# Interleaving gathered rounds and dense units by half rounds of four groups in a seven-pass graph network kernel

## The chip, the cores and the metric

The kernel runs as one program on one core of a Trainium2 chip. The metric is device time in microseconds (us) of one execution, the median of three runs. The engines are PE (matrix multiply), DVE (vector), ACT (scalar), POOL (gathers) and SP (issues transfers); each runs its own instruction stream and they meet at semaphores.

## The reference, cut to what matters

Four graph layers over 12500 nodes of 64 features and 200000 edges sorted by destination; each is followed by a residual and a layer norm:

```
x = _layernorm(x + L0(x))    # attention over edges, 4 heads
x = _layernorm(x + L1(x))    # per-node standard deviation of x[src]
x = _layernorm(x + L2(x))    # sum of x[src] + edges @ We, then an MLP
x = _layernorm(x + L3(x))    # four sage convolutions in a row
# sage_conv:
msg = x[src]
agg = jax.ops.segment_sum(msg, dst, num_segments=N_NODES)
deg = jax.ops.segment_sum(ones, dst, num_segments=N_NODES)
return (agg / maximum(deg, 1)) @ Wl.T + bl + x @ Wr.T
```

What the change touches is `segment_sum(x[src], dst)` in five passes: L1 ("dev") and the four convolutions ("sage1" to "sage4"). Destinations are crowded at low node numbers (`dst = 12500 * u**2`), so the upper half of the nodes receives only about 29% of the edges.

## The kernel before, in words

Nodes lie in 98 tiles of 128. Edges lie in 49 rounds of 8 groups of 512 edges. There are seven passes: gat, dev, gine, sage1, sage2, sage3, sage4. The passes gat and gine gather every round. Before dev, a matrix of edge counts (49 destination tiles by 98 source tiles, each 128x128, bf16) is built in DRAM.

The passes dev and sage1 to sage4 (`pass_dense`) work in two ways at once:

- **Dense unit.** For each of the 49 lower destination tiles, PE multiplies the 98 count tiles of that row by the node values (L921): 49 matmuls into one PSUM half (half 0), 49 into the other (half 1). SP keeps loading count tiles into a ring that holds exactly one unit, in 8 pieces; a piece is loaded again once its matmuls are done. DVE reduces each half (L1746) and adds it to the accumulator (L1750), in `take_dense`. In dev the unit is 28 + 21 matmuls, and the units run a second time over the other half of the sources.
- **Gathered (cold) round.** The last 15 rounds, whose edges go to the upper tiles, are gathered by POOL with indirect transfers into 8 slots (L620). For every pair of a group and a destination tile, DVE makes a one-hot matrix (L1700), PE multiplies (L949, 12 matmuls) into one of two PSUM banks, and DVE adds the sum of the pair before (L1707). A slot is handed back by DVE's index copy (L1695). The 15 rounds have 169 pairs in each pass, so about 11 in a round.

The order of the two is written in the program and depends on tables in SBUF that DVE computes once (L1657 to L1674). The outer loop has 7 steps ("blocks") of 7 units; at its end two blocks of nodes are processed (`node_vector` on DVE, `node_tensor` on PE, normalisation and the rows for the next pass; in dev one). TARGETS says how many rounds must be done at the end of each step, TURNS how many are done before each unit. After every unit, PE and DVE each load two values of TURNS into registers (L430, L431) and run the rounds between them (`cold_rounds`). On DVE the rounds stand between half 0 and half 1 of a unit: `take_dense(t, u, 0)`, the rounds, `take_dense(t, u, 1)`. The first group of four in a round loads eight registers of group spans (L425), the fifth does so again.

With the gains of the steps of 3, 3, 2, 2, 2, 2 and 1 rounds, the runs of units between rounds are 3, 2, 2 in the first two steps, 4, 3 in the next four, and 7 in the last. The last round of a step stands directly before its node work.

Of the kernel before, what the change touches and what calls it, by code (L numbers as in the profile page):

```python
# [15 lines left out]
P = 128  # L16
# [9 lines left out]
C = 4  # L26
# [58 lines left out]
def build(nc, x, edge_attr, src_r, dst_r, dst_b, src_c, dst_c, w, out):  # L85
    ctx = ExitStack()
    with ctx:
# [159 lines left out]
        TURNS = sb("TURNS", [P, KT + 1], I32)  # L247
# [180 lines left out]
        def cold_rounds(eng, u, r0, cold_round):  # L428

            first = eng.value_load(TURNS[0:1, bass.ds(u, 1)], min_val=0, max_val=ROUNDS)  # L430
            upto = eng.value_load(TURNS[0:1, bass.ds(u + 1, 1)], min_val=0, max_val=ROUNDS)  # L431
            with eng.If(first < upto):
                with eng.Fori(first, upto) as l:
                    cold_round(nc.s_assert_within(l + r0, 0, ROUNDS - 1, skip_runtime_bounds_check_because="upto <= ROUNDS - r0"))
# [277 lines left out]
        def _(pe):  # L712
# [193 lines left out]
            arrived = pe.alloc_register("pe_arrived")  # L906
# [18 lines left out]
            def pass_dense(k):  # L925
# [5 lines left out]
                def cold_round(r):  # L931

                    pe.reg_add(arrived, arrived, 16 * C)
                    for s in range(SLOTS):
# [21 lines left out]
                if dev:  # L956
# [4 lines left out]
                    for half in range(2):  # L961
                        pe.wait_ge(xp_loaded, 16 * (xp_before[k] + half + 1))
                        with pe.Fori(0, KT) as u:
                            dense_unit(k, u, u + half * KT, SRC_HALF)
                            if half == 0:
                                cold_rounds(pe, u, r0, cold_round)
                    return
                pe.wait_ge(xp_loaded, 16 * (xp_before[k] + xp_loads[k]))
                with pe.Fori(0, STEPS) as b:
                    with pe.Fori(0, TB) as r:  # L970
                        u = b * TB + r
                        dense_unit(k, u, u, TILES)
                        cold_rounds(pe, u, r0, cold_round)
                    node_tensor(pe, k, b * 2)
                    node_tensor(pe, k, b * 2 + 1)
# [275 lines left out]
        def _(ve):  # L1251
# [319 lines left out]
            def build_vector():  # L1571
# [93 lines left out]
                shares = tmp[:, 0, 0:KT].rearrange("p (b r) -> p b r", b=STEPS)  # L1665
                shares_i = tmp[:, 1, 0:KT].bitcast(I32)
                for r in range(TB):
                    step(ve.tensor_scalar(shares[:, :, r], gain, float(r * 9363), None, ALU.mult))
                step(ve.tensor_copy(shares_i, tmp[:, 0, 0:KT]))
                step(ve.tensor_scalar(shares_i, shares_i, 16, None, ALU.arith_shift_right))  # L1670
                step(ve.tensor_copy(tmp[:, 0, 0:KT], shares_i))
                step(ve.tensor_tensor(shares, shares, TARGETS[:, 0:STEPS].unsqueeze(2).broadcast_to([P, STEPS, TB]), ALU.add))
                step(ve.tensor_copy(TURNS[:, 0:KT], tmp[:, 0, 0:KT]))
                step(ve.tensor_copy(TURNS[:, KT:KT + 1], TARGETS[:, STEPS:STEPS + 1]))  # L1674
# [8 lines left out]
            prev, after = ve.alloc_register("ve_prev"), ve.alloc_register("ve_after")  # L1683

            def pass_dense(k):
# [23 lines left out]
                def cold_round(r):  # L1709

                    for s in range(SLOTS):
# [42 lines left out]
                def unit(t, u, rounds):  # L1754

                    take_dense(t, u, 0)
                    if rounds:
                        cold_rounds(ve, t, r0, cold_round)
                    take_dense(t, u, 1)

                for s in range(SLOTS - 1):
                    take_indices(s, r0 * SLOTS + s)
                if name == "dev":
                    with ve.Fori(0, STEPS) as b:
                        step.loop(b, per + 1)
                        with ve.Fori(0, TB) as r:
                            unit(b * TB + r, b * TB + r, True)
# [3 lines left out]
                    with ve.Fori(0, STEPS) as b:  # L1771
                        step.loop(b, per)
                        with ve.Fori(0, TB) as r:
                            unit(b * TB + r, b * TB + r + KT, False)
# [58 lines left out]
```

## Time and profile before

| what | us |
|---|---|
| median of 3 runs | 12794.58 (12789.05 to 12804.66) |
| profiled execution | 12813.53 |
| its span | 12811.7 |
| dev, its first 49 units with the 15 rounds | 5829 to 6658 |
| sage1 / sage2 / sage3 / sage4 | 9189 / 10205 / 10979 / 11938 to the end |

The profile counts an engine busy only while it computes. Register loads, branches and semaphore waits are idle time: an idle stretch that ends with "issue" is one in which the engine's own sequencer was at work. A row of the timeline gives start, length, engine, line, operation, operands, count, and in brackets the idle time before it with what ended it.

### The profile page before, as it was taken

How to read it: one execution, taken by the hardware profiler on the slowest of the kernel's cores; microseconds unless marked ns; L12 is line 12 of the kernel's file. 1: busy time of each engine (PE TensorE's matmuls, PEld its weight loads, DVE VectorE, ACT ScalarE, POOL GpSimd, SP SyncE). 2: the span in 40 equal slices, each digit the busy share in tenths (PEclk: the TensorE clock that was granted, in tenths of full speed). 3: DMA queues.
4: the chain of work that ended last, by engine and by line, in shares of the span. 5: the costliest groups of instructions: out<-in, count | busy, mean ns of one | idle time of the engine just before them, and what ended most of it. 6: DMA issues, size and time to landing. Idle time of an engine off the chain costs nothing.

```text
span 12811.7 us, 273411 instructions
## 1 busy us (share of the span) xinstructions
PE 7656.7 (60%) x61727; PEld 5494.5 (43%) x61728; DVE 5118.7 (40%) x13474; ACT 1761.8 (14%) x3566; POOL 5615.3 (44%) x5555
## 2 busy tenths in 40 slices
PE   5666666663665555556788444444566655455666
PEld 4555555552112222224455333444555544444566
DVE  4444545546544444443433222333322233322333
ACT  2333333331012222330000000000000000000000
POOL 4666555452000000005530577777654376554554
PEclk7777777776555555557889655566677766666777
DMA  2222222221001111115555322222455566655666
GB/s 59 66 63 63 64 62 61 61 59 36 20 40 54 66 70 70 70 80 169 150 169 176 75 51 56 56 58 58 121 189 173 198 206 232 217 183 199 203 216 202
DMA packets 977744, 1416.34 MB, mean 111 GB/s; under 512 B 540705, under 2 KB 649761, under 8 KB 970914
## 3 DMA queue, kind: packets, MB, share of 16 engines
q1 hardware_dynamic: 689858, 1130.79, 26.0%
q0 software_dynamic: 184832, 224.29, 9.0%
q10 hardware_dynamic: 102752, 58.62, 1.6%
q14 instruction: 281, 2.30, 0.1%
q8 instruction: 21, 0.34, 0.0%
HBM read 1197.73 MB, written 215.36 MB: 110 GB/s over the span
## 4 chain that ended last, share of the span: by engine, by line
PE 31%; issue 23%; DVE 14%; DVEq 14%; POOL 9%; DMA 6%; ACT 1%; SPq 1%; POOLq 0%; ACTq 0%
PE ps_turn L921 13%; POOL ARENA L620 9%; PE ps_turn L884 7%; PE ps_out L776 4%; DMA ARENA<-table_gat,idx 2%; DMA ARENA<-counts 2%; DVE onehots L1700 2%; DVEq L1714 2%; PE ps_pair L776 1%; DMA idx<-src_r 1%; DVEq L392 1%; PE ps_turn L692 1%; PE ps_pair L949 1%; DVE ARENA L1635 1%; DVEq L1630 1%
## 5 line engine op out<-in xcount | busy, mean ns | idle before, releaser
L620 POOL DMA_INDIRECT ARENA<-table_sage,idx x1920 | 1901.7, 990 | 1729.5 <-DVE idx L1695 1192.8
L921 PE MATMUL ps_turn<-ARENA 128*128 128x96 bf16 (+2 forms) x24010 | 2274.4, 262 | 543.0 <-DVE DSUM L1746 215.9
L921 PEld LDWEIGHTS ps_turn<-ARENA 128*128 128x128 bf16 x24010 | 1864.0, 106 | 948.7 <-issue 647.7
L884 PE MATMUL ps_turn<-ARENA 128*128 x3736 | 1515.8, 508 | 1219.5 <-issue 584.4
L620 POOL DMA_INDIRECT ARENA<-table_gat,idx x1568 | 1671.9, 1066 | 1188.1 <-issue 1131.0
L620 POOL DMA_INDIRECT ARENA<-table_gine,idx x1568 | 1541.2, 983 | 964.1 <-issue 950.1
L620 POOL DMA_INDIRECT ARENA<-table_dev,idx x480 | 481.8, 1004 | 2660.0 <-DVE idx L1695 2522.3
L1635 DVE TENSOR_SCALAR ARENA<-ARENA 128x784 f16 x1868 | 902.6, 483 | 1415.9 <-PE ps_turn L884 963.9
L949 PE MATMUL ps_pair<-ARENA,onehots 128*128 128x32 bf16 (+2 forms) x10140 | 699.7, 227 | 997.4 <-DVE ARENA L1707 868.6
L776 PE MATMUL ps_out<-ARENA,onehots 128*128 128x256 f32 (+1 forms) x3136 | 950.0, 472 | 517.7 <-DMA ARENA<-table_gine,idx 368.9
L884 PEld LDWEIGHTS ps_turn<-ARENA 128*128 x3736 | 389.1, 104 | 1959.0 <-issue 1863.2
L776 PE MATMUL ps_pair<-ARENA,onehots 128*128 128x256 f32 (+1 forms) x3136 | 882.5, 446 | 389.1 <-DMA ARENA<-table_gine,idx 303.4
L949 PEld LDWEIGHTS ps_pair<-ARENA,onehots 128*128 x10140 | 574.0, 117 | 1128.3 <-issue 1127.1
L776 PEld LDWEIGHTS ps_out<-ARENA,onehots 128*128 128x128 f32 x3136 | 724.1, 286 | 631.5 <-issue 555.5
L1073 ACT ACTIVATE ARENA<-ps_turn 128x784 f32 x784 | 645.4, 823 | 2112.9 <-PE ps_turn L902 2112.9
L1746 DVE TENSOR_REDUCE DSUM<-ps_turn 128x128 f32<-128x384 f32 (+2 forms) x588 | 230.0, 391 | 1756.2 <-PE ps_turn L921 1643.5
L1700 DVE SCALAR_TENSOR_TENSOR onehots<-DST,TBASE,COL 128x512 f32 x845 | 637.0, 754 | 640.0 <-issue 639.5
L776 PEld LDWEIGHTS ps_pair<-ARENA,onehots 128*128 128x128 f32 x3136 | 677.8, 269 | 493.9 <-issue 429.3
L1030 ACT ACTIVATE bigT<-ps_turn 128x896 f32<-128x896 f32 (+1 forms) x42 | 38.4, 915 | 3454.3 <-PE ps_turn L685 3454.3
L1450 DVE TENSOR_TENSOR ARENA<-ARENA,ps_out 128x261 f32 (+1 forms) x584 | 205.7, 354 | 761.8 <-PE ps_out L776 761.3
L1018 ACT ACTIVATE tmp<-COL,dst_in 128x128 bf16<-128x128 f32 x1568 | 495.3, 386 | 0.0
L776 PE MATMUL ps_out<-ARENA,tmp 128*128 128x256 f32 (+1 forms) x1536 | 417.2, 435 | 128.0 <-DVE tmp L1444 126.2
(298 smaller groups left out, 6850.4 us busy)
## 6 DMA issues: line engine op xcount, KB each, us to landing
ARENA<-counts SPq DMA_DIRECT2D x1470, 448.0 KB
counts<-ARENA SPq DMA_DIRECT2D x49, 3136.0 KB, 9.0
ARENA<-counts SPq DMA_DIRECT2D x490, 224.0 KB
ARENA<-dst_b SPq DMA_DIRECT2D x393, 256.0 KB
ARENA<-edge_attr SPq DMA_DIRECT2D x390, 128.0 KB, 2.5
ARENA<-table_sage,idx POOLq DMA_INDIRECT x1920
ARENA<-table_gat,idx POOLq DMA_INDIRECT x1568
ARENA<-table_gine,idx POOLq DMA_INDIRECT x1568
```

Of the source, the lines that this page charges most:

```text
L620: pool.indirect_dma_start(ps["buf"][:, s, c, 0:ps["row"]], None, ps["table"][:, :], bass.IndirectOffsetOnAxis(idx[:, s, c:c + 1], 0)).then ...
L776: last = pe.matmul(sums[:, 0:H * D if gat else n], lhs, rhs, start=(c == 0 and q == 0), stop=(c == C - 1 and q == parts - 1))
L884: last = pe.matmul(ps_turn[:, at:at + WIDE_ROW // 2], ring[:, 0:P], ring[:, P + q * (WIDE_ROW // 2):P + (q + 1) * (WIDE_ROW // 2)], start= ...
L921: last = pe.matmul(ps_dense[half][:, 0:n], RING[:, b, :], XP[:, b, :], start=(b == PIECE_AT[pieces[0]]), stop=(j == pieces[-1] and b == PI ...
L949: last = pe.matmul(sums, hot[:, c * P:(c + 1) * P], buf[:, s, c, q * n:(q + 1) * n], start=(c == 0 and q == 0), stop=(c == C - 1 and q == 2))
L1018: act.activation(distance[:, c * P:(c + 1) * P], COL[:, :], ACT.Abs, scale=-1.0, bias=dst_in[:, s % 2, c:c + 1]).then_inc(hot_distance, 1)
L1073: act.activation(to[:, :, c * CHUNK:(c + 1) * CHUNK].rearrange("p (q b) v -> p q b v", q=2), sums.rearrange("p q (b v) -> p q b v", v=CHUN ...
L1450: return ve.tensor_tensor(a, a, ps_sums[q][:, 0:n].unsqueeze(1), ALU.add)
L1635: ve.tensor_scalar(ring[:, P:P + WIDE_ROW], IOTA16, BASES[:, bass.ds(i * 4 + c, 1)], KEY[:, bass.ds(j, 1)], ALU.add, ALU.is_equal).then_in ...
L1700: return ve.scalar_tensor_tensor(ring, DST[:, bass.ds(cols, C)].unsqueeze(2).broadcast_to([P, C, P]), TBASE[:, bass.ds(t, 1)], COL[:, :].u ...
L1714: with ve.Fori(lo, hi) as t:
L1746: ve.tensor_reduce(DSUM[:, half, 0:n], ps_dense[half][:, 0:3 * n].rearrange("p (q v) -> p v q", q=3), X_AXIS, ALU.add).then_inc(dense_read, 1)
```

## The change

`cold_rounds` is replaced by `dense_step`, which runs one outer step. TURNS has an entry for each half round (98 entries): how many units precede it. Each half round loads its entry, runs the units up to it, then runs four groups. The step starts by loading two entries of TARGETS_I and ends with the units that are left. On DVE a unit is now whole: both halves are taken, then come groups. By the new table the half rounds stand after 1, 2, 3, 4, 5 and 7 units in a step of 3 rounds, after 1, 3, 5 and 7 in a step of 2, and after 3 and 7 in a step of 1. There are thus 30 stretches of gathered work in a pass where there were 15.

```diff
-        def cold_rounds(eng, u, r0, cold_round):
-            first = eng.value_load(TURNS[0:1, bass.ds(u, 1)], ...)
-            upto = eng.value_load(TURNS[0:1, bass.ds(u + 1, 1)], ...)
-            with eng.If(first < upto):
-                with eng.Fori(first, upto) as l:
-                    cold_round(... l + r0 ...)
+        def dense_step(eng, b, done, r0, dense_unit, cold_groups):
+            def units(upto):
+                now = eng.snap(done, min_val=0, max_val=KT)
+                with eng.If(now < upto):
+                    with eng.Fori(now, upto) as u:
+                        dense_unit(... u ...)
+                    eng.reg_mov(done, upto)
+            first = eng.value_load(TARGETS_I[0:1, bass.ds(b, 1)], ...)
+            upto = eng.value_load(TARGETS_I[0:1, bass.ds(b + 1, 1)], ...)
+            with eng.If(first < upto):
+                with eng.Fori(first, upto) as l:
+                    for half in range(2):
+                        units(eng.value_load(TURNS[0:1, bass.ds(l * 2 + half, 1)], ...))
+                        cold_groups(r, range(half * SLOTS // 2, (half + 1) * SLOTS // 2))
+            units(b * TB + TB)
...
 # PE, in the outer loop over b (dev alike)
-                    with pe.Fori(0, TB) as r:
-                        u = b * TB + r
-                        dense_unit(k, u, u, TILES)
-                        cold_rounds(pe, u, r0, cold_round)
+                    dense_step(pe, b, done, r0, lambda u: dense_unit(k, u, u, TILES), cold_groups)
...
 # DVE
-                def unit(t, u, rounds):
+                def unit(t, u):
                     take_dense(t, u, 0)
-                    if rounds:
-                        cold_rounds(ve, t, r0, cold_round)
                     take_dense(t, u, 1)
...
 # the table, on DVE
-                for r in range(TB):
-                    step(ve.tensor_scalar(shares[:, :, r], gain, float(r * 9363), None, ALU.mult))
+                for b in range(STEPS):
+                    step(ve.tensor_scalar(shares[:, b, :], COL[:, 0:2 * ROUNDS], begin[:, b:b + 1], rate[:, b:b + 1], ALU.subtract, ALU.mult))
...
```

DVE, sage4, from the reading of the first half of a unit to the first load of a gathered round, before. DSUM is the reduced half, ps_turn the PSUM of the dense halves, SPAN the table of tiles of each group; piece_used_3 is signalled by PE at the end of half 0.

```order
1862 L1746 TENSOR_REDUCE DSUM<-ps_turn 128x64 [waits piece_used_3]
1863 L1747 ISA
1864 L1750 ISA [waits dense_read]
1865 L1750 SCALAR_TENSOR_TENSOR ARENA<-DSUM,FLAG,ARENA 128x64
1866 L1751 REGISTER_ALU
1867 L430 ISA [waits dense_added]
1868 L430 TENSOR_LOAD TURNS
...
1871 L431 TENSOR_LOAD TURNS
...
1876 L425 TENSOR_LOAD SPAN
```

The same place of the changed kernel; piece_used_7 is signalled by PE at the end of half 1.

```order
2045 L1768 REGISTER_ALU [waits dense_added]
2046 L1770 TENSOR_REDUCE DSUM<-ps_turn 128x64 [waits piece_used_7]
2047 L1771 REGISTER_ALU
2048 L1774 SCALAR_TENSOR_TENSOR ARENA<-DSUM,FLAG,ARENA 128x64 [waits dense_read]
2049 L1775 REGISTER_ALU
2050 L434 REGISTER_ALU [waits dense_added]
2051 L434 COMPARE_AND_BRANCH
2052 L433 UNCONDITIONAL_BRANCH
2053 L426 ISA
2054 L426 TENSOR_LOAD SPAN
```

Gathered work on DVE moved from behind the reading of half 0 to behind the reading of half 1, and the two loads of TURNS between are gone.

PE, sage4, from the last matmuls of a unit to the wait for the first one-hot, before. The semaphore pair_hot is signalled by DVE's one-hot, gathered_3_0 by the gather.

```order
1483 L921 MATMUL ps_turn<-ARENA 128x192 x6
1484 L430 ISA
1485 L430 TENSOR_LOAD TURNS
...
1488 L431 TENSOR_LOAD TURNS
...
1493 L425 TENSOR_LOAD SPAN
1494 L404 ISA
1495 L938 UNCONDITIONAL_BRANCH [waits gathered_3_0]
1496 L939 ISA
1497 L945 ISA [waits pair_hot,pair_acc]
```

The middle of a round in the changed kernel, where dense units now stand between the fourth group and the fifth:

```order
1781 L952 COMPARE_AND_BRANCH
1782 L445 ISA
1783 L445 TENSOR_LOAD TURNS
...
1785 L433 COMPARE_AND_BRANCH
1786 L434 UNCONDITIONAL_BRANCH
1787 L434 ISA
1788 L931 ISA [waits dense_read]
...
1806 L934 MATMUL ps_turn<-ARENA 128x192 x6
1807 L434 REGISTER_ALU
1808 L434 COMPARE_AND_BRANCH
...
1811 L426 TENSOR_LOAD SPAN
```

On PE the two loads after every unit are gone, and one load stands after every four groups.

## Rows read from the trace of the kernel before

**Rows 1.** The page: chain that ended last, by engine
```profile
PE 31%; issue 23%; DVE 14%; DVEq 14%; POOL 9%; DMA 6%; ACT 1%; SPq 1%; POOLq 0%; ACTq 0%
```

**Rows 2.** Windows: start:end, us, busy us (count) by engine, PEclk, DMA share, GB/s
```profile
5829.00:6658.00 829.00, 629.79 (x4429) 410.68 (x4427) 340.99 (x780) 4.71 (x12) 481.76 (x480) 0.82 0.54 160
...
10205.00:10979.00 774.00, 400.83 (x6830) 366.84 (x6827) 257.23 (x739) 13.27 (x42) 476.42 (x481) 0.69 0.66 228
```

**Rows 3.** Waits from 5829: who waited for whom, total, times, longest
```profile
PE ps_pair L949 <- DVE ARENA L1707: 868.6, 748, 3.3
```

**Rows 4.** Timeline of PE, sage4, two stretches of units and one round
```profile
12338.10 11.05 PE L921 MATMUL ps_turn<-ARENA 128*128 128x192 bf16 x98 [1.60 <-issue]
12353.36 9.90 PE L921 MATMUL ps_turn<-ARENA 128*128 128x192 bf16 x98 [4.21 <-DVE DSUM L1746]
...
12393.73 0.82 PE L949 MATMUL ps_pair<-ARENA,onehots 128*128 128x64 bf16 x12 [1.72 <-DVE ARENA L1707]
...
12404.63 10.24 PE L921 MATMUL ps_turn<-ARENA 128*128 128x192 bf16 x98 [1.21 <-issue]
12416.02 8.24 PE L921 MATMUL ps_turn<-ARENA 128*128 128x192 bf16 x98 [1.16 <-DVE DSUM L1746]
...
12435.69 0.73 PE L949 MATMUL ps_pair<-ARENA,onehots 128*128 128x64 bf16 x12 [2.04 <-issue]
```

**Rows 5.** Timeline of DVE, sage4, end of a unit and start of a round
```profile
12424.42 0.36 DVE L1746 TENSOR_REDUCE DSUM<-ps_turn 128x64 f32<-128x192 f32 x1 [3.16 <-PE ps_turn L921]
12424.92 0.28 DVE L1750 SCALAR_TENSOR_TENSOR ARENA<-DSUM,FLAG,ARENA 128x64 f32 x1
...
12430.36 0.28 DVE L1750 SCALAR_TENSOR_TENSOR ARENA<-DSUM,FLAG,ARENA 128x64 f32 x1 [0.24 <-DVE DSUM L1746]
12433.72 0.75 DVE L1700 SCALAR_TENSOR_TENSOR onehots<-DST,TBASE,COL 128x512 f32 x1 [3.07 <-issue]
```

**Rows 6.** The lines of the register loads: count, ns min/median/max
```profile
L430 DVEq FUSED_REGOPS  x490: 46/132/224, 5837.8 to 12769.9; - x164
...
L430 DVEq TENSOR_LOAD <-TURNS x245: 300/312/849, 5837.9 to 12769.6; - x123
...
L425 DVEq TENSOR_LOAD <-SPAN x150: 594/605/628, 5855.6 to 12783.2; - x150
```

**Rows 7.** Windows in sage4: a steady unit, a round, the start of the next units
```profile
12374.00:12384.00 10.00, 8.03 (x98) 7.80 (x95) 2.05 (x6) 0.00 (x0) 0.00 (x0) 1.00 0.96 315
12388.00:12404.00 16.00, 6.80 (x101) 5.40 (x98) 9.20 (x24) 0.00 (x0) 12.32 (x13) 0.50 0.18 37
12404.60:12409.60 5.00, 4.97 (x37) 4.66 (x38) 0.00 (x0) 0.00 (x0) 3.78 (x5) 0.58 0.38 93
```

**Rows 8.** Timeline of PE, dev, three units and a round
```profile
6280.19 24.85 PE L921 MATMUL ps_turn<-ARENA 128*128 128x384 bf16 x147 [0.45 <-issue]
6307.22 0.84 PE L949 MATMUL ps_pair<-ARENA,onehots 128*128 128x128 bf16 x12 [2.19 <-DVE ARENA L1707]
...
6319.92 1.46 PE L949 MATMUL ps_pair<-ARENA,onehots 128*128 128x128 bf16 x12 [1.75 <-DVE ARENA L1707]
```

**Rows 9.** Timeline of PE, sage3, two units between rounds
```profile
11181.76 6.67 PE L921 MATMUL ps_turn<-ARENA 128*128 128x96 bf16 x98 [1.35 <-issue]
...
11199.37 0.65 PE L949 MATMUL ps_pair<-ARENA,onehots 128*128 128x32 bf16 x12 [3.24 <-DVE onehots L1700]
```

**Rows 10.** Timeline of PE, sage3, first units of a step of four and three
```profile
11418.09 4.72 PE L921 MATMUL ps_turn<-ARENA 128*128 128x96 bf16 x98
...
11448.15 1.06 PE L921 MATMUL ps_turn<-ARENA 128*128 128x96 bf16 x21 [0.38 <-DMA ARENA<-counts]
```

**Rows 11.** Timeline of DVE before dev: the old table
```profile
5810.01 1.42 DVE L1668 TENSOR_SCALAR tmp<-small 128x7 f32<-128x7 f32 x7
```

**Rows 12.** DMA queues, gat (1000:1400): packets, MB, share
```profile
q14 instruction: 37, 0.30, 0.3%
```

**Rows 13.** DMA queues, sage2 (10205:10979)
```profile
q14 instruction: 4, 0.03, 0.0%
```

More of the change, by code:

```diff
@@ L246, in build @@
         INFO = sb("INFO", [P, 2], I32)
-        TURNS = sb("TURNS", [P, KT + 1], I32)
+        TARGETS_I = sb("TARGETS_I", [P, STEPS + 1], I32)
+        TURNS = sb("TURNS", [P, 2 * ROUNDS], I32)
         rangev = sb("rangev", [P, 2 * H])
@@ L905, in _ @@
             seen, turn, bank = pe.alloc_register("pe_pair"), pe.alloc_register("pe_turn"), pe.alloc_register("pe_bank")
-            arrived = pe.alloc_register("pe_arrived")
+            arrived, done = pe.alloc_register("pe_arrived"), pe.alloc_register("pe_done")
             def dense_unit(k, t, u, srcs):
@@ L929, in pass_dense, with cold_groups @@
                 dev = ps["name"] == "dev"
-                def cold_round(r):
-                    pe.reg_add(arrived, arrived, 16 * C)
-                    for s in range(SLOTS):
+                def cold_groups(r, slots):
+                    if slots[0] == 0:
+                        pe.reg_add(arrived, arrived, 16 * C)
+                    for s in slots:
                         lo, hi = load_four(pe, spans, s, r * SLOTS + s)
@@ L1683, in _ @@
             prev, after = ve.alloc_register("ve_prev"), ve.alloc_register("ve_after")
+            done = ve.alloc_register("ve_done")
             def pass_dense(k):
@@ L1707, in add, with cold_groups @@
                     return ve.tensor_tensor(a, a, ps_pair[:, bass.ds(ve.snap(bank, min_val=0, max_val=512), n)].unsqueeze(1), ALU.add)
-                def cold_round(r):
-                    for s in range(SLOTS):
+                def cold_groups(r, slots):
+                    for s in slots:
                         g = r * SLOTS + s
@@ L1762, in pass_dense @@
                     take_indices(s, r0 * SLOTS + s)
+                ve.reg_mov(done, 0)
                 if name == "dev":
@@ L1765, in pass_dense @@
                         step.loop(b, per + 1)
-                        with ve.Fori(0, TB) as r:
-                            unit(b * TB + r, b * TB + r, True)
+                        dense_step(ve, b, done, r0, lambda u: unit(u, u), cold_groups)
                         flush()
@@ L1773, in pass_dense @@
                         with ve.Fori(0, TB) as r:
-                            unit(b * TB + r, b * TB + r + KT, False)
+                            unit(b * TB + r, b * TB + r + KT)
                         node_vector(ve, step, k, split, b + STEPS, b)
@@ L1779, in pass_dense @@
                     step.loop(b, 2 * per + 1)
-                    with ve.Fori(0, TB) as r:
-                        unit(b * TB + r, b * TB + r, True)
+                    dense_step(ve, b, done, r0, lambda u: unit(u, u), cold_groups)
                     flush()
```

45 lines of the change are left out of this document (30 added, 15 removed).

## The prediction

> **What bounds the kernel now.** I read the chain that ended last first [rows 1]: PE has 31%, and issue and DVE's sequencer another 37%. No engine and no transfer is full, so time goes into hand-overs between PE and DVE. Then the windows by pass [rows 2]: in dev PE is busy 630 of 829 us, in sage2 401 of 774, and POOL, whose 480 gathers are the fixed work of a pass, 482 and 476. So POOL has some 300 us of idle time in either. In the list of waits [rows 3] PE's gathered matmuls wait for DVE's additions (868.6 us): PE and DVE take turns there at some 1.8 us a pair, and no gather is waited for. So the order of the work matters only through what a switch between dense and gathered work costs, and what it hides.
>
> The timeline of PE shows a switch [rows 4]. A steady unit of sage4 takes 8.24 us and the next starts 1.16 us later. After the last unit of a run the first gathered matmuls come 2.04 us later, and after a round the next unit comes 1.21 us later and takes 10.24 us instead of 8.24. DVE's side [rows 5]: it reads half 0, loads the table, and makes the first one-hot from 12433.72, while PE's unit runs to 12425.41 + 8.24 = 12433.65 (the unit after the row of 12416.02). The one-hot is done by 12434.47, PE is ready for it at 12435.69. The preparation of DVE is thus hidden behind half 1 of the unit. This cover the change takes away: DVE now reads half 1, which exists only when PE has stopped, before it makes the first one-hot.
>
> **The change part by part.** Per pass there are 30 stretches of gathered work where there were 15; 7 still end a step. All times are of the profiled execution.
>
> *Entry of a gathered stretch, after.* In sage4, from PE's end of the unit (T = 12416.02 + 8.24 = 12424.26): DVE starts the reduction at T + 0.16, and its addition ends at T + 0.94 [rows 5]. From that point to a one-hot it was 3.07 us of issue, in which stood two loads of TURNS. One is a load of 0.31 us, two register operations of 0.13 and the steps between, about 0.75 [rows 6]; without two of them 1.6 us are left. The one-hot takes 0.75, and PE needs about 0.5 from there to its first matmul. Sum 0.94 + 1.6 + 0.75 + 0.5 = 3.8 us, against 2.04. For dev, whose reduction and addition are 0.25 us longer together, 4.05 against 2.19 [rows 8]. For sage2 and sage3, with shorter ones, 3.65 against 3.24 [rows 9]. No row shows this entry as such. Below, it is no shorter than the old one, if something hides the chain; above, I allow 1.2 us more, which is the extra idle of DVE's path if the register work of the new loops is as long as that of a load pair. I take the sums, as each part has a row.
>
> *Exit.* One load of TURNS now stands behind every four groups: 1.21 + 0.75 = 2.0 us in the sage passes, 0.45 + 0.8 = 1.3 in dev [rows 4, 8].
>
> *Middle of a round.* It had an idle time of 1.72 us, in which both engines load spans [rows 4], 1.75 in dev [rows 8] (about 2.0 in sage3). A new switch replaces it, so it is subtracted.
>
> *Slow first unit.* [...] A half round with its two gaps is still some 14 us in which PE does little, so I charge the 2.0 us at each new switch. In dev three units of 49 + 49 half matmuls after a round took 24.85 us [rows 8], 0.8 above three times 8.0.
>
> New switches, 15 in each pass: sage1 and sage4 3.8 + 2.0 - 1.75 + 2.0 = 6.05, so 91 us each. Dev 4.05 + 1.3 - 1.65 + 0.8 = 4.5, so 68. Sage2 and sage3 3.65 + 2.1 - 2.0 = 3.75, so 56 each (their unit times come below).
>
> Old entries, 15 in each pass, grow by 1.8 (sage1, sage4: 27), 1.85 (dev: 28) and 0.45 (7). The 8 old exits inside steps grow by 0.75: 6 us a pass.
>
> *Start of a step.* Two loads of TARGETS_I and one of TURNS, 2.3 us on PE and on DVE, 7 times: 16 us a pass. Where PE's first unit is hidden behind DVE's node work (sage4: PE waits until 12353.36 [rows 4]) it is DVE's loads that count, and the price is the same.
>
> *What is saved.* Inside a run of units PE's pause of 1.16 us [rows 4] is mostly its two loads. There were 34 such pauses in a pass and are 19, which I put at 0.2: sage1 saves 35 us, sage4 27, since 7 of its pauses lie behind node work. In dev the pause does not show (24.85 for three units). In sage2 and sage3 the units of a long run wait for the ring: in sage3 four units took 31.1 us (11418.09 to 11449.2) [rows 10], the first of them 4.72 of computing, and two units between rounds 14.4 (11181.76 to 11199.37 - 3.24) [rows 9]. During a half round the ring fills, so a run of one costs 5.0 at the start of a step and 6.3 elsewhere (6.67 in the row), a run of two 14.4. A step of two rounds then has 5 + 3 x 14.4 = 48.2 where it had 31.1 and, for three units, a time between 31.1 and 14.4, about 24: 55. Four such steps save 28, the two of three rounds about 9 each: 46 us a pass. This is the one real gain, a fuller ring.
>
> *The table.* It took 2.8 us; seven operations of 0.20 [rows 11] stay seven, but several over 686 columns come in. I put 5 us (0 to 15), on the path before dev.
>
> Sum: sage1 91 + 27 + 6 + 16 - 35 = 105; sage4 113; dev 68 + 28 + 6 + 16 = 118; sage2 and sage3 56 + 7 + 6 + 16 - 46 = 39 each; table 5. Together 419 us. The profiled execution took 12813.5, so 13232; it was 0.15% above the median of the runs, so the time on their scale is 13213 us, 3.3% slower.
>
> **The rivals.**
> *A. Most of the chain stays hidden, or the clock holds.* If the entries stay as they were, the new and old ones together cost 2 x (27 + 27 + 28 + 7 + 7) = 192 us less: 13020. If the first units after a half round keep the high clock, as a shorter pause might allow, 72 us less: 13140. For it: the clock in the round of [rows 7] is low only because PE is nearly idle. Against: the dependence on half 1 is in the program's order.
> *B. Not slower.* The finer order fills the ring and spreads the gathers; every switch is free. Then what is left is the saving: 35 + 27 + 2 x 46 = 154 us against 80 for the steps' starts, 30 for the exits and 5 for the table, about 12760. It decides only if DVE had time to make the one-hot before PE ends half 1, and DVE cannot pass its own wait for half 1.
> *C. Code loading.* The block loop on DVE grows, since the unit stands in it three times. In the gat pass, whose loop on DVE is longer than that of any other pass, the instruction queue moved 37 packets in 400 us [rows 12]; in sage2, 4 in 774 us [rows 13]. If the new loop behaved as that of gat, each of the 35 steps would load anew, at a few packets and perhaps 2 to 4 us: 70 to 140 us more, 13280 to 13350.
> [...]
> *D. The table does not spread the half rounds*, for instance by its rounding. Then both halves follow one another and only the old entries, the loads and the table are paid: some 96 + 80 + 5 + 15 x 5 x 0.75 = 237, less 120 saved in pauses: 12920.
>
> [...]
>
> **How the numbers follow.** Forecast as summed 0.72, A 0.12 (between 13020 and 13140), B 0.04, C 0.07, D 0.05. The forecast's own error is a fifth of its 420 us, and the bounds of the entries (192 us down, 1.2 x 150 = 180 up) are rarely reached whole. The range is 13050 to 13350 us. About 0.2% is what a measurement of this kernel can tell from no change. Faster by more has 0.04 (B), within it 0.02 (a part of B or D), slower 0.94.
>
> **What would show it right or wrong.** Of the profile of the changed kernel I expect: 30 stretches of L963 in each pass; idle time of PE before the first of each of 3.6 to 4.1 us, ended by DVE's one-hot; in sage4 about 2 us before the units after it and 10 us for the first; runs of units with pauses near 0.2 in sage1; sage2 and sage3 longer by some 40 us, dev, sage1 and sage4 by 105 to 118. POOL's gathers stay 480 a pass and are hardly waited for. It is wrong if the entries stay near 2 us, if the first units after a half round take 8.2, if instruction packets appear in the sage passes, or if PE waits for gathers in the steps of three rounds, where four groups are asked for every 21 to 25 us (6.3 or 10.2 for the unit, a switch, half a round) and POOL has 16 us of work for them (16 gathers of 1.0 us, 482 over 480 in [rows 2]) besides its gaps.

## The result and the profile after

| | us |
|---|---|
| before, median of 4 runs | 12792.9 (12789.05 to 12804.66) |
| after, median of 4 runs | 13296.22 (13287.02 to 13300.2) |
| ratio after/before | 1.0391 (95% interval 1.0373 to 1.0409) |
| profiled span, before / after | 12811.7 / 13296.3 |

The change makes the kernel 3.9% slower. The forecast was 13213, 3.3%. The windows of the changed kernel, one for each pass (dev first half, dev second half, gine, sage1, sage2, sage3, sage4); the columns are those of [rows 2]:

```profile
5838.80:6815.00 976.20, 696.42 (x4429) 449.27 (x4430) 342.37 (x776) 4.70 (x12) 478.65 (x480) 0.73 0.45 135
6815.00:7293.00 478.00, 408.01 (x2402) 239.66 (x2402) 174.84 (x350) 6.28 (x16) 8.30 (x9) 0.92 0.57 169
7293.00:9361.30 2068.30, 952.00 (x4255) 828.00 (x4254) 620.98 (x1222) 50.96 (x84) 1546.37 (x1563) 0.58 0.26 58
9361.30:10467.50 1106.20, 709.86 (x7180) 629.41 (x7180) 289.22 (x753) 40.20 (x70) 471.64 (x482) 0.71 0.51 170
10467.50:11291.80 824.30, 412.39 (x6830) 378.11 (x6830) 256.20 (x739) 13.27 (x42) 476.15 (x481) 0.67 0.63 214
11291.80:12292.40 1000.60, 518.78 (x7180) 440.34 (x7181) 279.22 (x753) 47.97 (x70) 477.60 (x480) 0.65 0.54 184
12292.40:13296.00 1003.60, 605.26 (x6830) 562.95 (x6830) 323.15 (x815) 2.92 (x14) 478.41 (x478) 0.72 0.54 181
```

The same windows of before are 829.2, 482.0, 2049.2, 1015.6, 774.2, 959.0 and 873.0 us. So dev grew by 147, sage1 by 91, sage2 by 50, sage3 by 42, sage4 by 131. What runs ahead of dev took 10 more (5839 for 5829), but it takes between 5823 and 5842 in the profiles of the experiments on like chips, so the 5 us of the table can't be told. Gine, whose code is untouched, grew by 19. DVE and POOL are as busy as before (dev 341 and 482 in [rows 2]); PE is busier with the same number of matmuls, at a lower mean clock (0.73 in dev, where [rows 2] have 0.82). The rest is waiting. Two rows of the waits from 5839 on:

```profile
DVE DSUM L1770 <- PE ps_turn L934: 2147.9, 517, 10.4
PE ps_pair L963 <- DVE ARENA L1731: 1273.8, 749, 15.7
```

The second was 868.6 us in 748 waits [rows 3]. The first was, in the kernel before, from 5829 on:

```profile
DVE DSUM L1746 <- PE ps_turn L921: 1643.5, 446, 8.9
```

DVE waits 504 us more for PE, in 71 more waits, and PE 405 us more for DVE's additions, in as many waits as before. The timeline of PE in sage1, one full cycle of a half round and two units, answers to [rows 4]:

```profile
10210.96 0.82 PE L963 MATMUL ps_pair<-ARENA,onehots 128*128 128x64 bf16 x12 [1.16 <-DVE ARENA L1731]
10213.40 18.12 PE L934 MATMUL ps_turn<-ARENA 128*128 128x192 bf16 x196 [1.63 <-issue]
10235.33 0.82 PE L963 MATMUL ps_pair<-ARENA,onehots 128*128 128x64 bf16 x12 [3.81 <-DVE ARENA L1731]
10236.90 0.82 PE L963 MATMUL ps_pair<-ARENA,onehots 128*128 128x64 bf16 x12 [0.74 <-DVE ARENA L1731]
```

The entry is 3.81 us (forecast 3.8, before 2.04), and the exit 1.63 (forecast 2.0, before 1.21). The exit differs from place to place: the next one in the same view is 2.07, and the median of sage1 is 1.62. Two units take 18.12 as one run without a pause between them. DVE's side of the same entry answers to [rows 5]:

```profile
10231.67 0.36 DVE L1770 TENSOR_REDUCE DSUM<-ps_turn 128x64 f32<-128x192 f32 x1 [3.29 <-PE ps_turn L934]
10232.18 0.28 DVE L1774 SCALAR_TENSOR_TENSOR ARENA<-DSUM,FLAG,ARENA 128x64 f32 x1
10234.11 0.75 DVE L1724 SCALAR_TENSOR_TENSOR onehots<-DST,TBASE,COL 128x512 f32 x1 [1.65 <-issue]
```

PE ends its unit at 10213.40 + 18.12 = 10231.52. DVE starts the reduction 0.15 later, ends the addition at + 0.94, issues for 1.65 (forecast 1.6), and the one-hot takes 0.75; PE starts at + 3.81. This chain lay behind half 1 before.

### The profile page after: what moved, and what is told of

Same layout as the page of the kernel before. It is cut to its first block, busy times and chain, and to the rows that moved or that the text cites. A ratio compares the mean times of both kernels' runs of the same rounds, so it can differ in the third digit from the quotient of the medians.

```text
span 13296.3 us, 271981 instructions
## 1 busy us (share of the span) xinstructions
PE 7812.0 (59%) x61727; PEld 5616.2 (42%) x61728; DVE 5118.0 (38%) x13480; ACT 1761.9 (13%) x3566; POOL 5623.4 (42%) x5555
## 4 chain that ended last, share of the span: by engine, by line
PE 33%; issue 23%; DVE 14%; DVEq 13%; POOL 9%; DMA 6%; ACT 1%; SPq 1%; POOLq 0%; ACTq 0%
PE ps_turn L934 14%; POOL ARENA L633 9%; PE ps_turn L897 7%; PE ps_out L789 4%; DMA ARENA<-table_gat,idx 2%; DMA ARENA<-counts 2%; DVE onehots L1724 2%; PE ps_pair L963 2%; DVEq L1738 2%; PE ps_pair L789 1%; DMA idx<-src_r 1%; PE ps_turn L705 1%; DVE ARENA L1650 1%; DVEq L393 1%; DVEq L1645 1%
## 5 line engine op out<-in xcount | busy, mean ns | idle before, releaser
L934 PE MATMUL ps_turn<-ARENA 128*128 128x96 bf16 (+2 forms) x24010 | 2387.7, 270 | 535.4 <-issue 366.0
L934 PEld LDWEIGHTS ps_turn<-ARENA 128*128 128x128 bf16 x24010 | 1949.9, 109 | 963.3 <-issue 664.8
L963 PE MATMUL ps_pair<-ARENA,onehots 128*128 128x32 bf16 (+2 forms) x10140 | 741.0, 234 | 1324.0 <-DVE ARENA L1731 1273.8
L963 PEld LDWEIGHTS ps_pair<-ARENA,onehots 128*128 x10140 | 608.8, 121 | 1467.1 <-issue 1465.1
```

The costliest lines, as they stand in the source:

```text
L934: last = pe.matmul(ps_dense[half][:, 0:n], RING[:, b, :], XP[:, b, :], start=(b == PIECE_AT[pieces[0]]), stop=(j == pieces[-1] and b == PI ...
L963: last = pe.matmul(sums, hot[:, c * P:(c + 1) * P], buf[:, s, c, q * n:(q + 1) * n], start=(c == 0 and q == 0), stop=(c == C - 1 and q == 2))
```

## Experiments

On one of the chips that served, the kernel before takes 16110 us (15964 in a second set of runs) instead of 12793; the first five experiments ran there. The gathered stretches of every kernel are torn there by pauses that the first chip does not have: in the third kernel below, from dev's last dense matmul to the first of sage1, a stretch that is almost all of gine and its gathers, it takes 2810 us where the kernel before has 2077 on the first chip; dev's second run of dense units, in which POOL gathers nothing, takes 452 and 455. In the kernel with DVE's old table and new order (third below) DVE's timeline in sage4 and its waits show one of them and their sum:

```profile
15214.33 0.22 DVE L1707 TENSOR_TENSOR ARENA<-ARENA,ps_pair  x1 [8.10 <-remote]
```

```profile
DVE ARENA L1707 <- remote: 1404.3, 206, 15.2
```

In the third kernel's 45 stretches of sage2 to sage4 the mean idle time of PE is 1.0 us before the second and third pair, 1.6 before the fourth, 4.0 before the fifth and 6.2 before the ninth, where the kernel before has 1.0 to 1.5 before each of the second to tenth in the four sage passes on the first chip. The pauses thus come mostly from the fourth or fifth pair of a stretch on, so they weigh on long stretches more than on short ones, and a ratio from there can't be carried to another chip: two kernels ran on both, and had 0.9832 and 0.9967 of the kernel before there, 1.0128 and 1.0327 elsewhere. The idle times between single instructions can: the new entry in sage1 has a median of 3.81 there, in the kernel with shifted code, and 3.83 on the first chip. From these five I use those; the seven others ran on chips where the kernel before takes 12803 and 12812 us.

**Half 1 behind the groups again.** Table, loops and 30 stretches stay as changed; DVE reads half 1 of the last unit only after the four groups.

```diff
-                        units(eng.value_load(TURNS[... l * 2 + half ...]))
-                        cold_groups(r, ...)
+                        goal = eng.value_load(TURNS[... l * 2 + half ...])
+                        with eng.If(now < goal):
+                            with eng.Fori(now, goal) as u:
+                                halves(u, 0)
+                                with eng.If(u + 1 < goal):
+                                    halves(u, 1)
+                        cold_groups(r, groups)
+                        with eng.If(now < goal):
+                            halves(kept, 1)
```

> The changed kernel, but on DVE the second half of the last unit before each half round is read behind the four groups, as in the kernel before; a unit index is kept in a register for it, and the code of DVE grows a little. Theory (the uncovered preparation on DVE is the largest part): the gaps between the end of a unit and the first gathered matmuls fall from 3.7 to 4.1 us to about 1.2 us (PE's own loads alone), 150 times, some 390 us less than the changed kernel: about 12900 us, between 12850 and 12980. Rival (the finer grain itself costs, by slow first units and exits): the gaps fall but the time stays above 13150. Rival (code loading on DVE): instruction packets grow further and eat 50 us or more of the gain.

15832.03 us, ratio 0.9832 (0.9811 to 0.9852) on the slow chip, so the expected 12900 can't be judged here; the tenth experiment does it. The medians of the entries were 1.03 in dev, 0.50 in sage1, 1.65 in sage2 and sage3, 0.52 in sage4, below the expected 1.2 in three passes and above it in two.

**Both half rounds at one place.** The changed kernel with a table that gives both halves of a round the same number of units: 15 stretches.

```diff
+                step(ve.tensor_copy(pairs_of[:, :, 0], pairs_of[:, :, 1]))
```

> The changed kernel, but the table gives both halves of a round the same number of units, so 15 stretches of gathered work stand in a pass and the code is the same. Theory: each of the 15 saved switches gives back 5.8 us in sage1 and sage4 (entry 3.8, exit 1.8, slow first unit 2.0, less 1.75 of idle time inside the round), 5.4 in dev, 3.75 in sage2 and sage3, 370 us in all, less 92 us that the fuller ring had given: about 13020 us. Rival (the order on DVE and the new loads are nearly all of it): 13200 or more. Rival (the ring's gain is not real): 12930.

16218.08 us, ratio 1.0069 (1.0045 to 1.0094) there, which decides neither for the expected 13020 nor for its rivals. The 15 entries kept the new length: 4.12, 3.83, 3.72, 3.84 and 3.85 us. The length of an entry is therefore not a matter of how often it comes, and the table of the change does spread the half rounds (30 stretches against 15): rival D falls.

**The order on DVE alone.** The kernel before, in which DVE reads half 1 ahead of the rounds.

```diff
                     take_dense(t, u, 0)
+                    take_dense(t, u, 1)
                     if rounds:
                         cold_rounds(ve, t, r0, cold_round)
-                    take_dense(t, u, 1)
```

> The kernel before, whole rounds and its own table, but DVE reads both halves of a unit before the rounds. Theory: the entry becomes 0.94 + 3.07 + 0.75 + 0.5 = 5.3 us in sage4 where it was 2.04, 3.3 us more 15 times in sage1, sage4 and dev, 1.9 more in sage2 and sage3: 206 us, about 13000 us. Rival (DVE's order is hidden by something else): within 30 us of the kernel before, 12793.

16295.88 us, ratio 1.0117 (1.0087 to 1.0147) there, which is 186 us. The medians of the entries are 5.50, 5.38, 5.12, 5.14 and 5.24, where the kernel before has 2.19, 2.04, 3.24, 3.23 and 2.02 on the first chip. The 75 entries add up to 396 us instead of 189, and the difference of 207 meets the expected 206; the time of the whole agrees, as far as a time from this chip can. One line that moves costs that much: with the two loads of TURNS still in the chain, an entry is 5.1 to 5.5 us; without them, as in the change, 3.8.

**Shifted code.** The changed kernel with 191 more instructions (semaphore increments) in a branch of DVE's program that is never taken, ahead of the building of the tables, so that DVE's loops from dev on stand 196 instructions further.

```diff
+                with ve.If(wide(ve) > 0):
+                    for _ in range(191):
+                        settle(ve)
```

> The changed kernel with 191 instructions on DVE that are never run (they stand in a branch that is not taken), ahead of the table building, so that all later loops of DVE stand elsewhere in the code. Theory (code loading is a part, which depends on where a loop stands): the 72 instruction packets of the gine pass and the 35 of sage4 go or change, gine falls by 19 us to the 2049 us that it took before, sage4 by up to 17: about 13260 us. Rival (gine and sage4 are longer for another reason): 13296 us, gine 2068, whatever the packets do.

16052.76 us, ratio 0.9967 (0.9955 to 0.9978) on the slow chip, where I had no run of the unchanged kernel to hold beside it: undecided. The instruction queue moved 285 packets where the changed kernel moves 379 and the kernel before 281.

**The loops with whole rounds and half 1 behind the groups.** The first two edits together, as a version that might beat both kernels.

> The changed kernel with the table of whole rounds (both halves of a round after the same units, so 15 stretches of gathered work) and, on DVE, the second half of the last unit before a round read behind its first four groups. The runs before this one had gaps at the entry of gathered work of 0.5 us with that cover (1.65 in sage2 and sage3), 3.8 without, where the kernel before has 2.0 (3.2). Theory (the hand-overs are the price, so whole rounds with the cover keep the saving of the loads and pay nothing): against the kernel before the entries give back 1.5 us 75 times (110 us), the pauses between units 60 us, and the starts of steps and the exits cost some 100 us: about 12720 us on a scale where the kernel before takes 12793, ratio 0.994 (0.985 to 1.003). Rival (the longer code of DVE or its branches eat it): a ratio of 1.005 or more.

15861.46 us, ratio 0.9945 (0.9927 to 0.9963). This met the number, but on the slow chip, and this kernel ran on no other. The half rounds with the same cover had 0.9832 there and 1.0128 elsewhere, so the number is not to be carried.

**The changed kernel again.** Unchanged, as the base for the next three.

> The changed kernel itself, unchanged, beside the kernel before on the chip on which the experiments run; it is the base for the others. On the first chip it took 1.0391 of the kernel before. If the pauses that stretch gathered work on the second chip fall on it as on the variant with the same half rounds (541 us against 1337 to 1444 us in the kernels with whole rounds), the ratio here is about 1.00 (15930 + 485 - 800 to 900 us: 0.97 to 1.00). If they do not depend on how long a stretch is, it is 1.03. Either way the medians of the entries should be 3.8 us in sage1 and sage4, 4.1 in dev, 3.7 in sage2 and sage3, and against the variant in which DVE reads half 1 behind the groups this one should be longer by the entries: some 30 x (2.2 x 2 + 3.0 + 2.0 + 3.3 - 2 x 0.5) or, from the medians of both, 30 x (3.1 + 3.3 + 2.1 + 2.1 + 3.3) = 417 us, less what the pair stretches took longer there (half 1 is still computing when the first pair comes), 200 to 300 us net.

13298.06 us (13283.93 to 13302.08) against 12803.36, ratio 1.0387 (1.0369 to 1.0404). This chip behaves as the first one; the ratio was expected for the slow one, and only the entries can be compared: 4.10, 3.82, 3.68, 3.75 and 3.82, as expected.

**Busier gathered stretches.** Three matmuls of 256 columns behind each pair, into a bank whose content is dead.

```diff
                             last.then_inc(pair_agg, 1)
+                            for _ in range(3):
+                                pe.matmul(ps_turn[:, 0:256], ZERO[:, :], ZEROS[:, 0:256], ...)
```

> The changed kernel with three more matmuls of 256 columns into a dead PSUM bank behind each pair on PE, so that PE is busier in a gathered stretch; nothing else is changed and the result of the extra work is not used. Theory (the slow first unit is the price of PE's idleness in the half round): the granted clock in the stretches rises, the first unit after a half round takes 8.3 instead of 10.5 us in sage1 and sage4 and about 8 instead of 10.2 in dev, and 5.9 instead of 6.1 in sage2 and sage3, so 90 x 2.1 = 190 us less, against at most 845 pairs x 0.3 to 0.6 us if the extra matmuls delay the next pair: between -190 and +300 us. Rival (the first unit is slow for another cause, such as count tiles that come late): its time stays at 10.5 and the kernel only gets longer by what the extra matmuls take. The length of a one-unit run is read in the trace, whatever the sum.

13199.61 us (13180.02 to 13206.26), ratio 1.0311 (1.0293 to 1.0328): 98 us less than the changed kernel in the same set. By pass dev gave 57, sage1 17, sage4 17, gine 7, sage2 and sage3 5 and 4. The first unit after a half round, median of all in a pass, fell from 10.01 to 8.12 us in dev, from 10.55 to 9.90 in sage1, from 10.29 to 9.90 in sage4 (9.93, 10.56 and 10.33 in the first profile of the changed kernel); in sage2 and sage3 it stayed at 6.2 to 6.4. The medians hide two kinds of units: 21 of 29 in dev and 9 of 29 in sage4 took 8.1 to 8.2 us, the others 9.4 to 11.0. So the expected 8.3 of sage1 and sage4 came for a part of the units alone, and 98 us of the 190 were won. A half round of dev and the first 3 us of the unit behind it, in the changed kernel:

```profile
6261.00:6273.00 12.00, 7.63 (x72) 6.16 (x72) 5.80 (x14) 0.00 (x0) 6.71 (x7) 0.64 0.15 41
6273.20:6276.20 3.00, 3.00 (x10) 1.46 (x11) 0.00 (x0) 0.00 (x0) 2.29 (x3) 0.50 0.29 86
```

The same with the three matmuls:

```profile
6443.00:6454.20 11.20, 8.11 (x75) 6.48 (x75) 4.60 (x11) 0.00 (x0) 8.27 (x8) 0.75 0.23 60
6454.30:6457.30 3.00, 3.00 (x19) 1.83 (x20) 0.00 (x0) 0.00 (x0) 2.09 (x4) 1.00 0.24 68
```

In 3 us PE does 10 matmuls at a granted clock of 0.50 and 19 at 1.00. The slow first unit is the clock: if the time of a first unit is multiplied by the mean granted clock in it, the product is 8.06 to 8.13 us for every one in dev and 8.14 to 8.25 for every one in sage1 and sage4, in the kernel before, in the changed one and with the matmuls, and PE has no idle time in one. Count tiles that come late would show as idle time, as the 0.38 before a run of 21 matmuls in [rows 10]. In sage2 and sage3 the product is 4.1 to 4.2 where the median unit takes 6.2 to 6.5, so the clock costs some 2.1 us there too, and with the three matmuls the clock of those half rounds was still 0.51 and 0.52 on average. The 57 us of dev are 41 less in the dense runs and 18 less in the gathered runs, with some 1 more in the idle times between them.

**The same in the kernel before.**

> The kernel before with the same three extra matmuls behind each pair. By the clock theory the first unit after a round falls from 10.24 to about 8.3 us in sage1 and sage4, 15 times in each, so half as much is won as in the changed kernel (some 60 to 90 us) at the same price for the pairs; the changed kernel gains by its larger number of first units. By the rival nothing is won.

12755.67 us (12745.58 to 12766.53, 6 runs), ratio 0.9962 (0.9949 to 0.9974): the only version that beats the kernel before on such a chip. A round of sage4 and the first 5 us of the unit behind it, and that unit in PE's timeline:

```profile
12388.00:12409.90 21.90, 15.06 (x177) 9.72 (x175) 11.92 (x32) 0.00 (x0) 15.20 (x15) 0.69 0.20 58
12410.00:12415.00 5.00, 5.00 (x61) 5.00 (x62) 4.21 (x8) 0.00 (x0) 3.92 (x4) 1.00 0.48 149
```

```profile
12305.41 10.13 PE L921 MATMUL ps_turn<-ARENA 128*128 128x192 bf16 x98 [7.01 <-DVE DSUM L1748]
...
12409.99 8.24 PE L921 MATMUL ps_turn<-ARENA 128*128 128x192 bf16 x98 [1.23 <-issue]
```

8.24 us instead of the 10.24 of [rows 4], at a clock of 1.00 instead of the 0.58 of [rows 7]. The price of the cold clock in a first unit was 2.0 us, as charged. In dev all 14 first units behind a round took 8.1, in sage4 8 of 14 took 8.2 and the others 9.7 to 10.6. The 48 us won are less than the 60 to 90 expected. Sage4 won only 6 us (dev 22, sage1 26), though its 14 first units had shrunk by 1.4 on average: behind node work PE arrives earlier and waits longer for DVE, 7.01 in the first row where [rows 4] have 4.21.

**Shifted code, beside the changed kernel.** The same kernel as the fourth, now in one set with its base.

> The changed kernel with 191 vector instructions in a branch that is never taken, ahead of the gine pass, so that the loops of gine and of sage1 to sage4 stand 196 instructions further in DVE's program; run once more, beside the unchanged kernel on the same chip. Theory (gine's 19 us more and a part of sage4's come from instructions loaded anew in every trip of a loop of about 300 instructions, 5 packets a trip, which depends on where the loop stands): gine is 15 to 25 us shorter than in the unchanged kernel, sage4 10 to 30 us, the instruction queue moves some 95 packets less, in all 20 to 50 us. Rival (gine's 19 us are something else, such as data that come later): the packets go and the time stays within 10 us.

13224.75 us (13215.62 to 13228.24), ratio 1.0327 (1.031 to 1.0344): 73 us less than the changed kernel, more than the 20 to 50 expected. The two profiled executions are 59 apart, of which gine is 20, sage4 36 and dev 7; dev has 2 instruction packets in both, so its 7 are not code loading. The instruction queue over the whole kernel, changed and then shifted:

```profile
q14 instruction: 379, 3.10, 0.1%
```

```profile
q14 instruction: 285, 2.33, 0.1%
```

In gine alone it was 69 packets, and 3 when shifted; in sage4 32, and 2. DVE's timeline at the start of a step of sage4 shows what they cost: the last operation of the node work and the next reduction, in the changed kernel of this set:

```profile
12448.59 0.62 DVE L1150 TENSOR_TENSOR X<-tmp,small 128x448 f32 x1
12460.98 0.36 DVE L1770 TENSOR_REDUCE DSUM<-ps_turn 128x64 f32<-128x192 f32 x1 [11.77 <-issue]
```

and shifted:

```profile
12426.63 0.62 DVE L1150 TENSOR_TENSOR X<-tmp,small 128x448 f32 x1
12430.82 0.36 DVE L1773 TENSOR_REDUCE DSUM<-ps_turn 128x64 f32<-128x192 f32 x1 [3.57 <-issue]
```

The same instructions, 8.2 us apart; PE had ended both halves of the unit at 12450.44 in the changed kernel, 10.5 us before the reduction. PE's first pair behind them shows it as an entry, changed and then shifted:

```profile
12465.92 0.82 PE L963 MATMUL ps_pair<-ARENA,onehots 128*128 128x64 bf16 x12 [15.48 <-DVE ARENA L1731]
```

```profile
12435.74 0.82 PE L963 MATMUL ps_pair<-ARENA,onehots 128*128 128x64 bf16 x12 [7.18 <-DVE ARENA L1734]
```

**Half 1 behind the groups, on a chip without the pauses.** The same kernel as the first.

> The changed kernel, but DVE reads half 1 of the last unit behind the four groups again, as the kernel before did: same table, same loops, 30 stretches a pass. Theory (the entries are the largest part of the loss): the entries, 665 us in the five passes of the changed kernel, fall to some 170 (medians 1.0 in dev, 0.5 in sage1 and sage4, 1.7 in sage2 and sage3, 30 each, plus those behind node work), and 30 to 100 us come back because the first pairs run while half 1 is still computed; so 400 to 470 us less than the unchanged changed kernel: 12830 to 12900 us, a ratio of 1.003 to 1.008 to the kernel before. Rival (loads, switches and the clock are the larger part): above 13000 us.

12972.91 us (12961.37 to 12980.23) against 12811.65, ratio 1.0128 (1.0111 to 1.0144). It is 325 us shorter than the changed kernel (whose median is from another chip, on which the kernel before is 8 us shorter), outside the 400 to 470 expected, and under the 13000 of the rival. The medians of the entries are as expected (1.01, 0.49, 1.61, 1.63, 0.49), and their sum over the five passes fell from 662 to 319, not to 170. The missing part is behind node work: five entries each of 12 to 14 us in sage2 and sage4, and of 8 in dev. Sage2 has 34 instruction packets in this kernel, where the changed kernel has 4, and sage4 33, where it has 32; gine has 3 for 69 and is 10 us shorter. In sage2 DVE's timeline shows the same hole as above, and PE's the entry:

```profile
10394.47 0.39 DVE L1173 TENSOR_TENSOR tmp<-big 128x224 f32<-128x224 f32 x1
10406.34 0.26 DVE L1786 TENSOR_REDUCE DSUM<-ps_turn 128x32 f32<-128x96 f32 x1 [11.48 <-issue]
```

```profile
10410.31 0.65 PE L979 MATMUL ps_pair<-ARENA,onehots 128*128 128x32 bf16 x12 [13.57 <-DVE ARENA L1747]
```

So the edit gave back what it should in sage1 (1007, before 1016) and sage3 (959, before 959), and came with its own code loading in sage2, which stayed at 830. Of the 161 us above the kernel before, sage2 has 56, dev 44 (first units still 9.80 us), sage4 40.

**That with the three matmuls.**

> The kernel of the run before with three more matmuls of 256 columns into a dead PSUM bank behind each gathered pair; their result is not used. Theory of the clock: with short entries PE idles less between a unit and the pairs, so the clock holds in dev as in the kernel before with these matmuls (first unit 8.1 us) and in sage1 and sage4 too (8.3 to 8.6 instead of 9.9): 60 to 150 us less than without them, 12700 to 12820 us. Rival (they delay the pairs when these overlap with half 1): no gain or a loss.

12889.47 us (12875.71 to 12890.89), ratio 1.0057 (1.0041 to 1.0074): 83 us less, by the theory, though above its 12820 since the base was higher. The first unit is 8.12 in dev, 10.16 in sage1 and 9.71 in sage4, where the theory said 8.3 to 8.6. As without the cover, 9 of the 29 in sage4 took 8.2 and the others 9.5 to 11.1, so the short entries did not change that.

**The same with both half rounds at one place.**

> The loops of the change, both half rounds of a round at one place by the table, half 1 read behind the groups, and the three extra matmuls: the best of all parts by the runs so far. Without the extra matmuls it was 0.9945 of the kernel before; with them the kernel before was 0.9962 of itself. If both add up, 0.990 to 0.992: 12680 to 12700 us.

12907.44 us (12887.19 to 12912.47), ratio 1.0069 (1.0052 to 1.0086). The expectation failed: 0.9945 had been measured where long stretches are torn by pauses, and it was wrong to multiply it with a ratio from another chip. Sage2 is at 829 and has 34 instruction packets here too. Between the last two kernels, which differ in the table alone, whole rounds are 18 us slower than half rounds. So in these loops the spreading of the half rounds costs nothing. That is not to say that the split is free against the kernel before: these loops pass from one kind of work to the other in the middle of every round, whether units stand there or not. PE's idle time in the middle of a whole round has a median of 3.4 to 4.1 us here by pass, where the kernel before with the same matmuls has 1.3 to 1.6, and the gathered runs of the five passes add up to 193 us more.

## Why the prediction was right, and where its numbers were not

The side, the mechanism and the range held. The terms stand beside what PE's timelines show, as sums of the idle times and runs of a pass (after minus before, forecast in brackets, in us):

| | entries | exits and step starts | gathered runs | dense runs | pass |
|---|---|---|---|---|---|
| dev | +111 (89) | +41 (42) | -6 (-25) | 0 (+12) | +147 (118) |
| sage1 | +84 (84) | +31 (52) | -25 (-26) | -6 (-5) | +91 (105) |
| sage2 | +66 (62) | +50 (54) | -25 (-30) | -43 (-46) | +50 (39) |
| sage3 | +75 (62) | +35 (54) | -28 (-30) | -39 (-46) | +42 (39) |
| sage4 | +141 (84) | +48 (52) | -26 (-26) | -32 (+3) | +131 (113) |

In sage1 and sage3 a step starts behind node work of PE. That work and the idle time behind it (+15 in sage1, +3 in sage3) are left out of the columns, though the forecasts in brackets hold 16 for the starts of steps. The passes differ from the sums of the columns by up to 7. The entries of sage4 hold about 36 us of code loading: with the shifted code they are +105.

- *Entries.* The chain of four parts came out at 3.8 in sage1 and sage4 and 3.7 in sage2 and sage3, and the change of DVE's order made it (third experiment, with the old loads still in the chain). This was most of the loss: with half 1 behind the groups 325 us of the 495 are gone (the placement of the code changed as well, which gave 10 back in gine). Rival A falls: in the changed kernel the entries did not stay hidden, and the first units did not keep the clock.
- *Slow first unit.* The 2.0 us of sage4 was right and is the clock: in sage4 of the kernel before the 14 first units behind a round took 9.55 to 11.05 us, and each multiplied by the mean granted clock in it gives 8.14 to 8.19. The term that was mis-sized is dev's: 0.8 a unit, read from three units that followed a whole round. The medians over all first units are 9.05 before and 9.93 after, against 8.12 at the full clock. So 29 x 1.8 - 15 x 0.9 = 39 us stand where I had 12. In the same way dev's gathered runs hardly shrank (-6 for -25). My reading took the clock of dev's rounds to stay as it was; before, it was 0.67 on average between the first pair of a round and the next unit, after, 0.51. The total of dev's dense runs hid this growth, by the next point.
- *Entries behind node work.* In the steps of sage4 and dev whose first stretch follows the first unit, that unit now runs while DVE still works on the nodes, and PE waits at the pair instead of at the next unit: 7.2 to 8.7 in sage4 without code loading, 7.4 to 8.7 in dev. The wait thus moved from the dense runs to the entries: sage4 has -32 for +3 there, and dev 0, though its first units alone added 39.
- *Fuller ring.* The one gain, -46 in sage2 and sage3, measured -43 and -39.
- *Code loading.* I had made it a rival of 0.07 and put it into each of the 35 steps at 2 to 4 us, for 13280 to 13350 us. The 37 packets of [rows 12] lie in seven rounds of gat (224 of its 1568 gathers), so 5.3 to a round, and by their share, 0.3% of 16 engines' 400 us, one took some 0.5 us, 2.6 a round. That a step would take 2 to 4 us longer was an estimate, and no run shows it: the first entry of five steps of sage4 took 14.4 to 15.5 us where it takes 7.2 to 8.7 with the shifted code, 5.9 to 8.3 more each, gine 20 us more over its 49 rounds, and dev, sage1, sage2 and sage3 have 2 to 4 packets each. The measured 13296 lies in that range and not at the forecast. It came, but in gine, which the change doesn't touch, and in sage4: 73 us by the shifted kernel. "It is wrong if instruction packets appear in the sage passes" did happen in one of them. Without it the kernel takes 13224.75 beside a kernel before of 12803, where the sum said 13213 beside 12795. That it comes so near is luck in part, since the errors of the passes cancelled: with the shifted code dev was forecast 22 too low and sage2 15 too low, sage1 15 and sage4 21 too high. The 83 us by which the forecast missed are almost wholly this rival.

In sage4 of the changed kernel 32 packets stand beside a hole of 11.77 us at the head of a step; with only the place of the code changed it is 2 packets and 3.57 us. My own reading of [rows 12] and [rows 13] went by the length of a loop alone, and failed there: gine's code is the same in all three kernels, only its place in the program changed, and it moved 3 packets in the kernel before, 69 in the changed one and 3 with the shifted code.

What stays open: why the three matmuls hold the clock in sage4 for 8 of 14 first units over whole rounds and for 9 of 29 over half rounds, and not at all in sage2 and sage3; what the pauses of the slow chip are; and which positions of a loop in the program load anew. Those were not tried.

## What to carry to other kernels

Before splitting a stretch of work, write down the chain from the last instruction of the one kind to the first of the other on both engines, and ask what it is hidden behind; here one line, the reading of half 1 ahead of the gathered groups, took the cover away; to put it back was worth 325 us over 150 entries. A term read from one place at one clock was good for that place only: dev's first units, charged 0.8 us from one place, were 0.9 above their 8.12 at the full clock in the kernel before and 1.8 in the changed one, as the clock of the gathered work ahead of them went from 0.67 to 0.51. Take the mean over all such places, and read the clock ahead of each. A median over units of two kinds misleads in the same way: count the kinds. After any edit of a long program, compare the packets of the instruction queue pass by pass, in the passes that were not touched as well.

## What was not expected of the hardware

- Moving DVE's loops by 196 instructions, with nothing else changed, was worth 73 us of 13298 (0.55%): 94 packets of the instruction queue, some 7 us at the first entry of each of five steps of sage4, and 20 us in gine.
- Matmuls without any use made the kernel before 0.38% faster (0.9962, interval 0.9949 to 0.9974), since they keep PE's granted clock at 1.00 for the first unit after a round, in dev each time and in sage4 8 times in 14.
- One chip ran the same kernels slower by a fifth to a quarter (16110 against 12793 us for the kernel before, 15832 against 12973 for half 1 behind the groups), with pauses of several us in gathered stretches (8.10 in the one shown). A ratio from it did not hold elsewhere: half 1 behind the groups was 0.9832 of the kernel before there and 1.0128 on another chip.
